# Two-layer network on one core: scattered sums in DRAM, a split down projection, and two stages dealt anew

## The reference

```
h = _gelu(einsum('td,edf->tef', xt, Wu)); y = einsum('tef,efd->ted', h, Wd)
moe = einsum('ted,te->td', y, cw)          # cw: the two weights of a token, else 0
x2 = x + mixer_scale * (r * wkv @ Wo.T)
h = leaky_relu(_rms(x2) @ Wfc.T, 0.5);  x3 = x2 + mlp_scale * (h * h @ Wmlp.T)
```

## Time and profile before

| | us |
|---|---|
| median of 3 runs | 2112.03 |
| profiled execution, its own time | 2117.18 |
| its span, first to last instruction | 2115.4 |
| TensorE busy, mean granted clock | 1739.3 (82%), 0.889 |
| VectorE, ScalarE, GpSimd busy | 1202.9, 881.9, 599.5 |

### The profile page before, as it was taken

The page is one execution under the profiler, slowest core; times in us unless marked ns, Lnnn a source line. Parts: engine busy times, 40 slices in busy tenths (PEclk is TensorE's granted clock), DMA queues, the critical chain, the costliest instruction groups (busy, mean ns, idle before and its releaser), DMA issues. The chain is left out here.

```text
span 2115.4 us, 36910 instructions
## 1 busy us (share of the span) xinstructions
PE 1739.3 (82%) x12492; PEld 1390.0 (66%) x12493; DVE 1202.9 (57%) x2736; ACT 881.9 (42%) x1739; POOL 599.5 (28%) x765
## 2 busy tenths in 40 slices
PE   5759999999994798699999387758887399999970
PEld 4625766666672477577887144457886399999970
DVE  4557677777733766333332488546664655555546
ACT  3200666666682264332232144433442044444336
POOL 1330011111113387423222644122221122312114
PEclk9955899999996599899999699979998599999995
DMA  5694233333303561122222421050001333322206
GB/s 200 245 145 56 53 78 73 76 73 77 75 13 103 172 229 70 50 64 71 64 62 62 142 69 56 0 202 21 21 11 63 100 106 123 108 84 72 77 9 238
DMA packets 142011, 191.00 MB, mean 90 GB/s; under 512 B 70465, under 2 KB 105123, under 8 KB 140864
## 3 DMA queue, kind: packets, MB, share of 16 engines
q1 hardware_dynamic: 113280, 131.79, 20.2%
q0 software_dynamic: 20992, 51.80, 9.0%
q10 hardware_dynamic: 7616, 5.77, 1.5%
HBM read 125.98 MB, written 65.54 MB: 91 GB/s over the span
## 5 line engine op out<-in xcount | busy, mean ns | idle before, releaser
L583 DVE TENSOR_REDUCE att_neg_max<-att_m_ps 128x1 f32<-128x320 f32 x496 | 234.7, 487 | 129.9 <-PE att_m_ps L410 122.3
L410 PE MATMUL att_m_ps<-att_k,att_q 96*128 96x384 f32 x496 | 229.3, 474 | 28.4 <-DMA att_k<-qk 21.0
L1827 PE MATMUL silu_h_ps<-silu_xT,silu_w_part 128*128 128x320 f32 x1536 | 237.9, 312 | 6.4 <-DVE silu_h L1935 3.2
L1827 PEld LDWEIGHTS silu_h_ps<-silu_xT,silu_w_part 128*128 128x128 f32 x1536 | 227.7, 189 | 9.4 <-issue 4.1
L410 PEld LDWEIGHTS att_m_ps<-att_k,att_q 96*128 96x128 f32 x496 | 103.6, 209 | 137.3 <-DVE att_neg_max L583 87.6
L1612 PE MATMUL gelu_y_ps<-layer_wd,gelu_hT 128*128 x576 | 138.0, 382 | 7.8 <-issue 7.1
L548 ACT ACTIVATE att_prob_f<-att_b_ps 128x1024 f32<-128x1024 f32 x64 | 65.6, 1024 | 172.6 <-PE att_b_ps L434 172.6
L2380 PE MATMUL mlp_y_ps<-mlp_wm_part,mlp_h_part 128*128 128x256 f32 x768 | 108.9, 311 | 28.2 <-DVE mlp_h_part L2491 28.2
L2380 PEld LDWEIGHTS mlp_y_ps<-mlp_wm_part,mlp_h_part 128*128 128x128 f32 x768 | 107.3, 220 | 30.4 <-DVE mlp_h_part L2491 30.4
L1573 POOL DMA_INDIRECT gelu_x<-rows,gelu_row_no x72 | 71.7, 996 | 173.7 <-PE gelu_x_ps L1584 156.5
L1612 PEld LDWEIGHTS gelu_y_ps<-layer_wd,gelu_hT 128*128 128x128 f32 x576 | 103.8, 190 | 23.3 <-issue 12.0
(11 more groups left out here) (313 smaller groups left out, 3825.3 us busy)
## 6 DMA issues: line engine op xcount, KB each, us to landing
experts_w<-in_dram SPq DMA_DIRECT2D x24, 1024.0 KB
qk<-qkv_part POOLq DMA_DIRECT2D x32, 512.0 KB, 3.3
att_k<-qk SPq DMA_DIRECT2D x192, 64.0 KB, 2.3
att_q<-qk SPq DMA_DIRECT2D x168, 64.0 KB, 3.0
expert_rows<-gelu_y SPq DMA_DIRECT2D x72, 128.0 KB, 1.7
expert_rows<-mlp_zero SPq DMA_DIRECT2D x8, 1024.0 KB, 16.5
v<-qkv_v POOLq DMA_DIRECT2D x8, 544.0 KB, 4.8
att_v<-v SPq DMA_DIRECT2D x8, 544.0 KB, 4.2
```

What stands on the lines that cost most here:

```text
L410: nc.tensor.matmul(bank[:, 0:2 * LOCAL].rearrange("p (a n) -> p a n", a=2), q[b][0:MROW, x, :], local_and_global(b, x), start=True, stop=T ...
L583: ins = nc.vector.tensor_reduce(neg_max[p % 2][:, x:x + 1], m_ps[u % 2][:, 0:LOCAL + 2 * BLK], AX.X, ALU.max, negate=True)
L1827: mm = nc.tensor.matmul(h_ps[u % 2][a][:, :], w12_part[f % RING][wp][:, a, k, :], xT[s][xp][:, k, rows], start=(i == 0), stop=(i == 3 * KD ...
```

## The change

1. **Scattered sums.** Every expert tile's output is multiplied by the slot's weight (`share`) and added into DRAM by an accumulating indirect DMA, into `part` in layer 0 and into `summed` in layer 1. Each waits for the one before to land. `gather_pairs`, `add_pairs`, the 8 MB fill and `combine` go; `mix_tokens` loads `part` alone, and `last_norm` loads `summed` alone. `mix_channels` stores its output twice (`rows[1]` and `summed`). `summed` is 4 MB.
2. **Tables.** `route` now also gives each slot's weight: `in_tile` has three columns (token number, high and low part of the weight), so the product L1501 makes three times as many elements, and the product L1215 streams three times as many columns.
3. **Gelu experts.** Up weights are split while tiles 0 to 4 use whole operands, down weights while tiles 0 to 7 do; one piece per tile on ScalarE and VectorE. From tile 8 on, `down` is 12 fp32r products. Gathers are issued one by one, six tiles ahead, between the scatters. There are 4 y buffers.
4. **Token mixing.** One load per group, three buffers; the two inverse roots come from one variance; the normalised input is made on ScalarE; the second normalisation is not applied to the rows: `x2` itself is turned, and its inverse mean square (`share`) scales the output of the channel mixing. All engines' orders are written anew.
5. **Channel mixing.** The downs of group g-1 stand between the ups of group g (after hidden tiles 2, 4, 5, 7), with two sets of `h_part`; additions take `share`.
6. All loops are written out (no `Fori`).

```diff
-def skewed(eng, first, last, step, start=2):
-    with eng.Fori(start // 2, NGRP // 2 - 1) as i:
+def skewed(first, last, step):
+    for g in range(first, NGRP + last):
+        step(g, g % 2)
...
# route
+                mm = nc.tensor.matmul(table_ps[:, r % 2:r % 2 + COLS - 1, :], in_slot[half % HALVES][:, r // 2, r % 2, :],
+                                      in_tile[half % HALVES][:, r // 2, r % 2, :, :], start=False, stop=False, ...)
+                spread = [P, 2 * N, COLS - 1, NT]
+                nc.vector.tensor_tensor(in_tile[...], is_tile[...].broadcast_to(spread), entry[...].broadcast_to(spread), ALU.mult)
...
# experts_gelu, GpSimd
+            for n in range(XS + 2):
+                gather(n)
+            for n in range(NT):
+                if n + XS + 2 < NT:
+                    gather(n + XS + 2)
+                pool.wait_ge(y_ready, n + 1)
+                if n > 0:
+                    pool.wait_ge(y_out, 16 * n)
+                nc.gpsimd.indirect_dma_start(out=sum_d, out_offset=bass.IndirectOffsetOnAxis(ap=table[:, 0, n:n + 1], axis=0),
+                                             in_=y[n % YS][:, :], in_offset=None, bounds_check=T - 1, oob_is_err=False,
+                                             compute_op=ALU.add).then_inc(y_out, 16)
# experts_gelu, TensorE
-            pe.wait_ge(wu_low, len(wu_pieces))
+                if n < FULL_UP:
+                    products = [(x_whole[s], wu, k) for k in range(KD)]
+                else:
+                    products = [(xT[s][xp], wu_part[wp], k) for k in range(KD) for xp, wp in TERMS]
+                if n < FULL_DOWN:
+                    products = [(hT_whole[s], wd, k) for k in range(KF)]
+                else:
+                    products = [(hT[s][hp], wd_part[wp], k) for k in range(KF) for hp, wp in TERMS]
# experts_gelu, VectorE, per tile
+                low_h(n, n % 2)
+                if n + 2 < NT:
+                    take_x(n + 2, n % 2)
+                take_y(n, n % 2)
+                low_piece(n)
...
# experts_silu
-                    nc.gpsimd.indirect_dma_start(out=y_d, ..., bounds_check=2 * T - 1, oob_is_err=False)
+                    nc.gpsimd.indirect_dma_start(out=sum_d, ..., bounds_check=T - 1, oob_is_err=False, compute_op=ALU.add)
...
# mix_tokens, TensorE
+            def step(g):
+                turn2(g - 1, 0)
+                project(g + 1, 0, 0), project(g + 1, 0, 1), project(g + 1, 0, 2)
+                turn2(g - 1, 1)
+                mix(g)
+                project(g + 1, 1, 0), project(g + 1, 1, 1)
+                turn1(g + 2, 0), turn1(g + 2, 1)
+                project(g + 1, 1, 2)
...
# mix_channels, TensorE
+            for g in range(NGRP + 3):
+                for f in range(KF):
+                    if exists(g):
+                        up(g, f)
+                    if exists(g - 1) and f in AFTER:
+                        down(g - 1, AFTER.index(f))
+                    if exists(g - 2) and f == KF - 2:
+                        norm.turn(pe, g - 2, g % 2)
...
# last_norm (in place of combine): 8 loads of 512 KB on the queues of SyncE and ScalarE; per group
+                    nc.vector.bn_stats(part[:, t, :], x[:, t, :])       # 4, then 4 bn_aggr
+                nc.scalar.activation(group(std, g), ..., ACT.Sqrt, bias=eps[:, 0:1])
+                    nc.scalar.activation(out[:, t, :], x[:, t, :], ACT.Identity, bias=shift[:, t:t + 1], scale=inv[:, t:t + 1])   # 4
```

More of the change, by code:

```diff
@@ L218, in _ @@
             pool.wait_ge(ones_set, 1)
-            with pool.Fori(0, NGRP) as i:
+            for i in range(0, NGRP):
                 for j in range(4):
@@ L911, in step, with last_norm @@
                     norm.copy(act, g - 1, 1 - s)
[L913 to L919, removed]
+            skewed(0, 1, step)
+def last_norm(nc, sum_d, out_d):
     with ExitStack() as ctx:
         m = Mem(nc, ctx, "combine")
[L922 to L928, removed]
+        x = m.sb("x", [P, TT, D])
+        out = m.sb("out", [P, TT, D])
+        part = m.sb("part", [P, TT, 6])
+        mean_var = m.sb("mean_var", [P, TT, 2])
+        std, inv, shift = (m.sb(a, [P, TT]) for a in ("std", "inv", "shift"))
@@ L956, in _ @@
[L956 to L966 removed]
+                sp.dma_start(token_rows(out_d, g), out[:, g * GT:(g + 1) * GT, :]).then_inc(stored, 16)
@@ L1070, in route @@
-def route(nc, tag, xT, Wg, bg, ident, upto, capacity, weight, pos, table, tile_expert, prefetch, shared=None):
+                act.wait_ge(shift_done, g + 1)
+                for t in range(g * GT, (g + 1) * GT):
+                    nc.scalar.activation(out[:, t, :], x[:, t, :], ACT.Identity, bias=shift[:, t:t + 1],
+                                         scale=inv[:, t:t + 1]).then_inc(normed, 1)
+def route(nc, tag, xT, Wg, bg, ident, upto, capacity, table, share, tile_expert, prefetch, shared=None):
@@ L1577, in _ @@
+            pool.wait_ge(y_out, 16 * NT)
         @block.tensor
@@ new lines, in _ @@
+            high_n(0)
+            for g in range(NGRP + 3):
+                for f in range(KF):
+                    i = g * KF + f
+                    if i < NGRP * KF:
+                        halve(i)
+                    if 0 < i <= NGRP * KF:
+                        square(i - 1)
+                    if f == 1 and exists(g + 1):
+                        high_n(g + 1)
+                    if f == 2 and exists(g - 2):
+                        norm.root(act, g - 2, g % 2)
+                    if f == KF - 1 and exists(g - 2):
+                        norm.copy(act, g - 2, g % 2)
@@ new lines, in add @@
+            def add(g, j):
+                t = g * GT + j
+                dve.wait_ge(y_done, t + 1)
+                nc.vector.scalar_tensor_tensor(out[g][:, j, :], y_ps[j % 2][:, :], share[:, t:t + 1], x[:, t, :],
+                                               ALU.mult, ALU.add).then_inc(summed, 1)
+            low_n(0)
+            for g in range(NGRP + 3):
+                for f in range(KF):
+                    i = g * KF + f
+                    if i < NGRP * KF:
+                        leak(i)
+                    if 0 < i <= NGRP * KF:
+                        high_h(i - 1)
+                    if exists(g - 2):
+                        if f == 1:
+                            norm.stats(dve, g - 2, g % 2)
+                        if f == 3:
+                            norm.apply(dve, g - 2, g % 2)
+                    if f == 4 and exists(g + 1):
+                        low_n(g + 1)
+                    if exists(g - 1) and f in AFTER:
+                        add(g - 1, AFTER.index(f))
```

1120 lines of the change are left out of this document (501 added, 619 removed).

## The result

The changed kernel takes 2059.07 us (median of 4 runs, 2057.57 to 2065.23) against 2112.16 us (4 runs, 2108.09 to 2113.32): ratio 0.9758, 95% interval [0.9734, 0.9781]. It is 53 us faster; 105 us were forecast (2007). The time lies inside the stated range (1970 to 2072), but half of the expected gain is missing. The profiled execution took 2058.43 us, its span is 2056.7.

The account below looks back on a forecast made before the run. No single engine bounds the kernel; each stage has its own limit. Terms +13-35-46-27+7+3-20 = -105 from 2117.2 us profiled give 2012, or 2007 for the median; range 1970 to 2072 us.

Parts of the forecast that it names:

- the gelu term's round trip: Gelu experts: each accumulating scatter waits for the last, 3.6 us a tile, near plain scatters; stage 274 us, -35.
- The bounds, 3.3 and 6.1: Gelu scatter round trip: 3.3 us as plain, 6.1 if destination rows are fetched first; term ends -47 and +145.
- its own mark (4.5): Sign against the forecast: gelu scatters lying 4.5 us apart or more.
- rival A: Scatter's round trip takes the gelu stage: 2200 us at 6.1; decides faster or slower at 5.0; chance 0.12.
- Rival C: New orders do not help: token mixing gains only start and tail (-22), channel mixing nothing; 2058 us; chance 0.13.
- C = 5.6: Gelu scatter round trip if all 2.3 us between issue and landing doubled; term +109, whole 2161 us.
- TensorE's floor: Gelu experts: TensorE's share of a tile falls from 3.86 to 3.37 us with the split down product.
- The start and end: Gelu experts: up(0) at about 4 us; sum takes 5 us before and 10 behind 72 tiles at 3.6.
- Token mixing: Term -46: TensorE becomes the limit, 17 us a group, first projection about 1183; ends -58 (floor 16) and -20.
- Channel mixing: Term -27: 24.5 us a group over a floor of 23.5, VectorE late next; ends -36 and -10.
- Route 0: Route of layer 0, +13: L1501 from 1.22 to 3.7 us in 8 bursts, two thirds of 19.6 showing.
- silu experts: Term +3: only the last five scatters show, at their round trip instead of 2.9 us; ends 0 and +16.

Follow-up runs that it names:

- Experiment 2: Changed kernel with the gelu stage's scatters writing instead of adding, so the sum is left out: 1983.59 us (one run).
- experiment 7: Kernel before, two separate edits: TensorE's gelu loop written out, 2124.69 us, ratio 1.0015; gathers one by one instead of by fours, 2104.33 us, ratio 0.9912.
- Experiment 5: Changed kernel with gelu scatters to two arrays in turn, joined in token mixing by VectorE instead of GpSimd, 1999.04 us, or by accumulating load, 1999.76 us.
- experiment 6: Changed kernel with channel mixing's four downs of the group before in a row after the last up, not between the ups: 2083.78 us (one run).
- experiment 4: Gelu down products all on whole operands: in the changed kernel 2055.03 us; in the two-array kernel with VectorE adding the arrays 2006.7 us.

## Why the prediction was right and wrong

- **The step that failed is the gelu term's round trip, "I take 3.6".** It is 4.65 in steady work, 4.73 on the mean: +80 us over 71 intervals. The mechanism was named, with the wait, the queue behind it and the sum for a longer C; the value was wrong. The bounds, 3.3 and 6.1, held; the choice by the nearest row (plain scatters) assumed that an add costs nothing to issue and little to land, for a reason (the reads overlap) that no row showed. Experiment 2 gives +0.55 us of issue and +1.3 us to landing (the issue in it). At 4.7 the forecast is declared wrong by its own mark (4.5); rival A turned out true in kind, short of its point of decision, 5.0.
- **Luck in the number.** Rival C names 2058 us, and 2059 was measured, but by the opposite road: C has both mixing stages keep their pitch and the gelu stage gain, where the mixing stages gained 97 us together and the gelu stage lost 52. The match supports nothing of C.
- The rule quoted beside it, from the Trainium skill's "Collectives: The Full Stack" ("Why ReduceScatter is half of AllGather"), that an add in a DMA costs twice the source reads, was used to double the time from issue to landing, C = 5.6. Here it grew from 2.5 to 3.8 us. The 2.3 us that were doubled are GpSimd's whole idle time between two plain scatters and hold the 0.85 us behind the landing too. From the issue's end to the landing it is 1.5 us plain and 2.2 with the add. Neither "free" nor double is what a dependent scatter pays.
- **TensorE's floor was also too low:** 3.37 us against 3.62. 1.92 us of busy time a tile was set against 1.42 of products, both by durations that overlap the next instruction; the starts give 1.73 and 1.52. And the tile it started from, 3.86 us of TensorE, held the late gathers of experiment 7; without them it is 3.77, and 3.77 less 0.16 is the 3.62 measured. Even with no chain the stage would be 290 us, not 262 or 274.
- **The start and end:** 15.8 us to the first scatter and 8.9 behind the last, 25 against the 19 in the sum. The first up product came 5 us into the stage, near the 4 said, but the first tile's passage from up to scatter was reckoned as one tile time. Beside VectorE's pieces two scatters took 2.8 and 3.4 us to issue, behind them 1.57, and their two intervals together are 4 us longer. One of them, and the piece (changed kernel):

```profile
912.62 2.28 DVE L1637 TENSOR_TENSOR gelu_wd_low_part<-layer_wd,gelu_wd_high_part 128x2048 fp32r<-128x2048 f32 x1
912.94 3.44 POOL L1501 DMA_INDIRECT part<-gelu_y,all_table  x1 [0.95 <-DVE gelu_y L1621]
```

  The piece ends at 914.90 and the issue 1.48 us after it. All six issues that start inside a piece end so: the two scatters 1.48 and 1.51 us after its end, the four gathers 0.87 us after it, about as long as an undisturbed issue takes (1.57 and 0.95 to 0.99). Those that start before a piece are not longer. The issue is held until VectorE's instruction is through. The Trainium skill ("SBUF — State Buffer", the warning on DMAs issued from GpSimd) describes such a held issue, but for VectorE's 2-port modes; of `tensor_tensor`, which the pieces are, the same page ("Who interferes with whom") says that it did not stall DMAs in a probe, and infers that it takes only the read side of the shared ports. Here indirect issues are held beside it, and the measurement decides. Whether they are held while they read their row numbers from SBUF, a read that the page would let it block, no run shows.
- The new gathers, which the prediction listed with no gain, are worth 16 us where TensorE sets the tile (experiment 7). In the changed kernel the scatters' chain sets it, and no run shows that they saved anything there.
- **Token mixing** (-60, where -46 was taken and -58 was the better end) was right in cause: TensorE is busy 91.55 of 92.4 us between 1255.6 and 1348 at clock 1.00 (changed kernel, first row below). Its group is 15.66 us, where 17 was taken and 16 called the floor, an estimate; the first projection came 12.3 us into the stage, as said. Experiment 5 shows how thin VectorE's slack is.
- **Channel mixing** came out at 23.4 us a group, the floor (23.5), where 24.5 was taken; the cause was right only in part. The reason given, that with the downs a group behind VectorE's chain has a whole group's time, is worth 0.9 of the 4.7 us by itself. That VectorE would be late next did not happen, but only because the downs are dealt out (experiment 6).
- **Route 0:** the threefold product takes 2.50 us, not three times the 1.22 of the earlier trace rows (changed kernel, VectorE's groups in route 0, in the fence below); so 8 bursts grew by 10 us instead of 20. Two thirds of that, the share that the prediction took, would be the 7 measured; no run tests the share. Route 1 and the last norm came within 2 us; the silu experts are 3 us shorter where 3 longer was taken, and no run says why.

A window of token mixing, and VectorE's costliest group of route 0, of the changed kernel:

```profile
1255.60:1348.00 92.40, 91.55 (x326) 52.71 (x325) 73.07 (x177) 64.53 (x141) 19.87 (x24) 1.00 0.07 23
```

```profile
L1432 DVE TENSOR_TENSOR route_in_tile<-route_at_tile,route_entry 128x1728 fp32r<-128x1728 f32 x8 | 20.0, 2496 | 0.0
```

## What to carry to other kernels

A chain of dependent accumulating scatters runs at its own round trip, here 4.65 us for 128 rows of 1 KB, and a faster or slower product beside it changed nothing (experiment 4). Before counting on a faster product, look whether a second destination can let each scatter wait for the one before the last; here that made it 3.62, where TensorE is the limit. Take durations from start to start when instructions are pipelined; sums of busy time can overstate what an edit removes, here 0.5 for 0.16 us a tile. An engine busy 97% of a window may still stop at every fourth tile: list the starts of one repeating instruction and look at the gaps.

## What was not expected of the hardware

An accumulating indirect scatter costs GpSimd 1.57 us to issue against 1.02 for the same plain one, and lands 3.8 us after its start against 2.5; in the last tiles, taken to have no valid rows, it still takes 1.54 and about 2.7. In two arrays in turn, with some 0.2 us of overlap, they still land in 3.8. An issue that starts while VectorE runs a `tensor_tensor` of two SBUF operands (2.28 us) is held until that ends. GpSimd's addition of 128x1024 in SBUF took 2.3 us and stretched VectorE's 128x256 normalisation beside it from 582 to 1007 ns.

What stays open: how the landing behaves when two such scatters overlap for long; why some scatter intervals of the changed kernel reach 5.9 to 6.6 us outside the pieces (3 of 71); and how the 0.75 us of longer transfer divides between reading the destination and adding.
